# Turning the next chunk's embeddings at the end of the old chunk's last tile, at all three chunk borders of a DLRM interaction kernel

## What is computed

```python
e = stack([tbl_f[ids[:, f]] for f in range(39)], axis=1)          # x0: (512, 39, 16)
for W in (W0, W1):                                                # (1, 39*Hk, 128)
    Wr = W.reshape(39, Hk, 128)                                   # Hk = 39, then 128
    xk = einsum('bid,bjd,ijh->bhd', x0, xk, Wr)
    outs.append(xk)
z = sum(concatenate(outs, axis=1), axis=-1)                       # (512, 256)
h = relu([z, dense_ctx] @ W_top1 + b_top1)                        # 272 -> 512
h = relu(h @ W_top2 + b_top2)                                     # 512 -> 256
y = h @ W_top3                                                    # 256 -> 1
```

## Time and profile before

| | before |
|---|---|
| median of 3 runs | 365.79 us (365.4 to 366.7) |
| profiled execution, time | 365.56 us |
| profiled execution, span of the trace | 363.8 us |
| PE busy | 229.9 us (63%), 1673 matmuls |
| DVE busy | 164.8 us (45%) |
| ACT busy | 158.9 us (44%) |
| POOL busy (gathers) | 98.0 us (27%) |

### The profile page before, as it was taken

The page is one execution under the profiler, slowest core; times in us unless marked ns, Lnnn a source line. Parts: engine busy times, 40 slices in busy tenths (PEclk is TensorE's granted clock), DMA queues, the critical chain, the costliest instruction groups (busy, mean ns, idle before and its releaser), DMA issues.

```text
span 363.8 us, 4707 instructions
## 1 busy us (share of the span) xinstructions
PE 229.9 (63%) x1673; PEld 176.2 (48%) x1673; DVE 164.8 (45%) x333; ACT 158.9 (44%) x307; POOL 98.0 (27%) x107
## 2 busy tenths in 40 slices
PE   5311100010001001889998999989999999999997
PEld 4200000000000000746765887667688877788896
DVE  4440000000000100589897867979784867745411
ACT  4600000000000300488887757986856877666411
POOL 5777777777777730000000000000000000000000
PEclk9655555555555555699999999999999999999999
DMA  6800100000000000019100000000000000000000
GB/s 175 253 14 6 10 6 6 7 7 6 6 7 6 6 5 0 0 31 304 46 21 2 1 2 1 2 0 3 1 2 2 0 3 0 3 0 2 0 2 0
DMA packets 7834, 8.61 MB, mean 24 GB/s; under 512 B 2759, under 2 KB 5420, under 8 KB 7812
## 3 DMA queue, kind: packets, MB, share of 16 engines
q1 hardware_dynamic: 4516, 7.48, 7.2%
q0 software_dynamic: 3296, 0.85, 2.5%
HBM read 8.32 MB, written 0.00 MB: 23 GB/s over the span
## 4 chain that ended last, share of the span: by engine, by line
PE 48%; issue 35%; DVE 7%; ACT 7%; another core or an unknown queue 2%; DMA 1%; ACTq 0%; DVEq 0%
PE turn_bank L542 10%; PE g_bank L512 5%; PE pair_bank L455 5%; PE x_bank L479 5%; PE x_bank L482 4%; PE x_bank L481 4%; DVE onehot L791 3%; ACT prod_hi L1027 2%; DVE prod_lo L864 2%; PE x_bank L522 2%; PE turn_bank L580 2%; PE g_bank L706 2%; PE turn_bank L553 1%; ACT prod L1022 1%
## 5 line engine op out<-in xcount | busy, mean ns | idle before, releaser
L430 POOL DMA_INDIRECT emb<-tbl,ids_sb x103 | 97.8, 950 | 33.5 <-issue 31.1
L1022 ACT ACTIVATE prod<-pair_bank 128x512 f32<-128x512 f32 (+1 forms) x112 | 66.2, 600 | 43.0 <-PE pair_bank L455 38.7
L864 DVE TENSOR_TENSOR prod_lo<-prod,prod_hi 128x512 fp32r<-128x512 f32 x96 | 65.1, 686 | 2.6
L479 PE MATMUL x_bank<-prod_hi,pair_w_hi 128*128 128x512 f32 (+1 forms) x112 | 63.4, 566 | 2.0 <-DVE prod_lo L864 1.9
L1142 ACT ACTIVATE looked<-pair_bank 128x192 f32<-128x192 f32 x2 | 0.6, 328 | 104.4 <-remote 104.4
L808 DVE COPY_PREDICATED looked<-odd,pair_bank 128x192 f32<-128x192 int32 x2 | 0.6, 370 | 97.6 <-issue 97.6
L455 PE MATMUL pair_bank<-x,sel 117*128 117x512 bf16 (+1 forms) x112 | 42.8, 384 | 0.9 <-ACT x L1004 0.7
L542 PE MATMUL turn_bank<-g_sb,w_sb 128*128 128x128 f32 x312 | 42.3, 279 | 0.0
L542 PEld LDWEIGHTS turn_bank<-g_sb,w_sb 128*128 128x128 f32 x312 | 39.4, 192 | 3.0 <-issue 1.2
L1027 ACT ACTIVATE prod_hi<-prod 128x512 fp32r<-128x512 f32 x64 | 40.0, 625 | 0.1
L482 PE MATMUL x_bank<-prod_hi,pair_w_lo 128*128 128x512 f32 x96 | 38.1, 397 | 0.0
(11 more groups left out here) (143 smaller groups left out, 315.2 us busy)
## 6 DMA issues: line engine op xcount, KB each, us to landing
emb<-tbl,ids_sb POOLq DMA_INDIRECT x103
tab<-small SPq DMA_DIRECT2D x2, 560.0 KB
wt<-w_top SPq DMA_DIRECT2D x2, 512.0 KB, 4.4
tab<-small SPq DMA_DIRECT2D x1, 504.0 KB
wa<-pair_w_a SPq DMA_DIRECT2D x1, 448.0 KB
wb<-pair_w_b SPq DMA_DIRECT2D x1, 448.0 KB
wtd<-w_dense SPq DMA_DIRECT2D x1, 256.0 KB
dense_sb<-dense_t SPq DMA_DIRECT2D x1, 256.0 KB
```

Of the source, the lines that this page charges most:

```text
L430: pool.indirect_dma_start(out=emb[:, at:at + D], out_offset=None, in_=tables[f], in_offset=bass.IndirectOffsetOnAxis(ap=ids_sb[:, c * M + ...
L479: mm = pe.matmul(x1_banks[k % 2][:, :], pair_w_hi[p, t, :], hi(n), start=(t == 0), stop=(t == FULL))
L864: dve.tensor_tensor(lo(n), prod[rows, n % RING, :], prod_hi[rows, n % RING2, :], ALU.subtract).then_inc(lo_done, 1)
L1022: act.activation(prod[0:ROWS[t], n % RING, :], pair_bank[n % 2][0:ROWS[t], :], ACT.Square).then_inc(sq_done, 1)
```

## The change

`SEAMS`, `ended` and `seam` are gone, so that all borders are crossed alike. `SPLIT_AT` gets a row for each chunk that is prepared: for each of the two pieces the tile of the last block at which its first half and its second half are issued. For chunk 1 the large piece stays at tiles 4 and 5 and the small one goes to tile 6; for chunks 2 and 3 the large piece is issued at tiles 0 and 1 and the small one at tiles 3 and 4. The turn moves from the new chunk's first tile to the old chunk's last, behind that tile's select and one `layer1`. So it stands ahead of `layer1` of the old chunk's last four tiles; before, two of these stood ahead of it at borders 2 and 3, and all four at border 1. The copies of the turned x move along with it. At border 1 layer 2 of chunk 0 moves from the seam and the first two blocks of chunk 1 to its blocks 2 and 3.

```diff
-SEAMS = (1,)
-SPLIT_AT = (4, 6)
+SPLIT_AT = ((), ((4, 5), (6, 6)), ((0, 1), (3, 4)), ((0, 1), (3, 4)))
...
-            def seam(c):
-
-
-                n, k = c * NB * NT, c * NB
-                for m in range(n - LAG1, n):
-                    layer1(m)
-                    if m % NT in G_AT:
-                        contract_d(k - 2, G_AT.index(m % NT))
-                turn_x1(k - 1)
-                contract_d(k - 1, 0)
-                turn(c, 0)
...
                 late = 1 <= c < NCH and j == 0
                 if late and t == 0:
                     layer1(m)
                     layer1(m + 1)
-                    pe.wait_ge(x1_done, n // NT - 1)
-                    turn(c, 0)
-                    pe.wait_ge(xblk_done, n // NT)
-                    turn(c, 1)
-                    pe.wait_ge(sq_done, n - 1)
-                    turn(c, 2)
-                    layer1(m + 2)
                 if n < TILES:
                     select_pair(n)
                 if m >= 0 and (not late or t >= LAG1):
                     layer1(m)
-                if late and t == 1:
-                    layer1(m + 2)
+                if late and t in (1, 2):
+                    layer1(m + 1)
+                if c + 1 < NCH and j == NB - 1 and t == NT - 1:
+                    pe.wait_ge(x1_done, n // NT)
+                    turn(c + 1, 0)
+                    pe.wait_ge(xblk_done, n // NT + 1)
+                    turn(c + 1, 1)
+                    pe.wait_ge(sq_done, n)
+                    turn(c + 1, 2)
...
-                if c in SEAMS and 13 + 3 * (NT * j + t - LAG1) < M:
-                    layer2(c - 1, 13 + 3 * (NT * j + t - LAG1), min(16 + 3 * (NT * j + t - LAG1), M))
-                if j == 2 and c >= 1 and c not in SEAMS:
+                if j == 2 and c >= 1:
                     layer2(c - 1, 3 * t, 3 * t + 3)
...
(DVE)
-                for p in range(len(SPLIT_AT) - 1):
-                    if splits and t == SPLIT_AT[p]:
+                if splits and t == NT - 1:
+                    take_lo(n - 1)
+                for p in range(len(CUTS) - 1):
+                    if splits and t == SPLIT_AT[c + 1][p][0]:
                         split_rest(c + 1, CUTS[p], CUTS[p + 1])
-                    if splits and t == SPLIT_AT[p] + 1:
+                    if splits and t == SPLIT_AT[c + 1][p][1]:
                         split_lo(c + 1, CUTS[p], CUTS[p + 1])
                 if splits and t == NT - 1:
-
-                    take_lo(n - 1)
...
+                    keep_turned(c + 1)
...
(ACT)
-                    split_first(c + 1, *CUTS[-2:])
-                    split_second(c + 1, *CUTS[-2:])
-                    if c + 1 in SEAMS:
-                        keep_g(k, 0)
-                    else:
-                        round_hi(n)
+                    round_hi(n)
+                    keep_turned(c + 1)
```

More of the change, by code:

```diff
@@ L209, in build_tower @@
         h1_sum = sem("h1_sum")
-        gathered = [[sem(f"gathered{c}_{p}") for p in range(len(SPLIT_AT) if c else 1)] for c in range(NCH)]
+        gathered = [[sem(f"gathered{c}_{p}") for p in range(len(CUTS) - 1 if c else 1)] for c in range(NCH)]
         split_first_done = sem("split_first_done")
@@ L644, in step @@
                     layer1(m)
-                if late and t == 1:
-                    layer1(m + 2)
+                if late and t in (1, 2):
[7 more added lines that the diff above has]
+                    turn(c + 1, 2)
                 if t == 0 and n < TILES:
                     turn_x(n // NT)
-                if u == 0 and k >= 1 and not ended(k - 1):
+                if u == 0 and k >= 1:
                     turn_x1(k - 1)
-                if u in G_AT and k >= 1 and not ended(k - 1):
+                if u in G_AT and k >= 1:
                     contract_d(k - 1, G_AT.index(u))
@@ L919, in step @@
                     spread_x(k)
-                if t == 1 and k >= 2 and not ended(k - 1) and not ended(k - 2):
+                if t == 1 and k >= 2:
                     keep_g(k - 2, 0)
@@ L923, in step @@
                     relu1(c - 2)
-                if t == 4 and k >= 2 and not ended(k - 1) and not ended(k - 2):
+                if t == 4 and k >= 2:
                     keep_g(k - 2, 1)
@@ L1089, in step @@
                 tile(n)
-                if t == 3 and k >= 1 and not ended(k - 1):
+                if t == 3 and k >= 1:
                     keep_x1h(k - 1)
-                if t == 1 and k >= 2 and not ended(k - 1) and not ended(k - 2):
+                if t == 1 and k >= 2:
                     keep_g(k - 2, 0)
-                if t == 4 and k >= 2 and not ended(k - 1) and not ended(k - 2):
+                if t == 4 and k >= 2:
                     keep_g(k - 2, 1)
-                if t == 5 and k >= 1 and not ended(k - 1):
+                if t == 5 and k >= 1:
                     keep_x1(k - 1)
```

32 lines of the change are left out of this document (2 added, 30 removed).

## The result

The changed kernel takes **367.63 us** (median of 5 runs, 367.22 to 367.95), the kernel before 365.79 us. The ratio is 1.004, with a 95% interval of 1.0025 to 1.0054: slower by 1.8 us. The profiled execution took 367.22 us with a span of 365.4 us. In two of the measurements further down one run lay hundreds of us above the others (one of six of after_again, one of twelve of fill12), and in one of the kernel before at 381 us; such runs are left out.

The account below looks back on a forecast made before the run. The prediction took PE (TensorE) to set the pace inside the chunks. Terms of -1.9, -0.6, +2.1, +0.3, +0.3 and a last 0.2 summed to +0.4, forecasting 366.2 us, with a range of 364.9 to 368.3.

Parts of the forecast that it names:

- a clock under 1.00 behind the hole: Sign in the trace after, at border 1: TensorE's clock below full level there would prove the forecast wrong on its sum.
- the clock's rival: At border 1 PE's standing lets the clock fall; four us at half speed lose 2.0, giving 368.2 us; chance 0.2.
- the sum: All gains and losses at the borders and in chunk 1's blocks together: +0.4 us, giving 366.2 us.
- Borders 2 and 3: Early splits and the moved turn remove PE's whole loss at these borders: -1.9 us and -0.6 us.
- The hole: At border 1, PE stands 3.9 us ahead of the turn, waiting for the last split.
- Border 1 in all: Loss at border 1 of 4.7 us in place of 2.6, from the standing, refill and a small gap: +2.1 us.
- The refill term: Behind the turn at border 1, without layer 2 as cover, PE loses 0.7 us to late work (bounds 0 and 1.2).
- Chunk 1's blocks: Blocks 0 and 1 without layer 2 lose 0.3 us; blocks 2 and 3 with it lose 0.3 us.
- The last 0.2: An allowance of 0.2 us for splits that a tile somewhere waits for.
- The other signs: Wait 3.5 to 4.2 us; tile 35's select near 205.8, tile 55's 2.5 to 3 later; borders 2 and 3 3.2 to 3.4.
- Only the hole costs: Rival: ACT and DVE get ahead during border 1's standing, so refill and chunk 1's blocks lose nothing: 364.6 us; chance 0.12.
- The early splits don't help: Rival: borders 2 and 3 don't gain their 2.5 us, as selects or layer 1 still wait: 368.7 us; chance 0.08.

Follow-up runs that it names:

- after_again: The changed kernel unaltered, measured again beside other kernels on one chip: 368.31 us, ratio 1.0064 to the kernel before.
- fill12: The changed kernel with 12 extra matmuls, whose result nobody reads, ahead of the turn at border 1: 366.40 us, ratio 1.0015 to the kernel before.
- fill16: The changed kernel with 16 extra 512-column matmuls, whose result nobody reads, ahead of the turn at border 1: 366.10 us, ratio 1.0009 to the kernel before.
- order1: The changed kernel with layer 1 of tiles 24 and 25 ahead of the turn at border 1 and tile 26's directly behind it: 365.88 us.
- fill8: The changed kernel with 8 extra matmuls, whose result nobody reads, directly behind layer 1 of tile 23: median 367.97 us, ratio 1.0053 to the kernel before.
- split5: The changed kernel with chunk 1's small split at tile 5 instead of 6: 234.93 us against 234.31 for the kernel before (shorter start-up), ratio 1.0011.
- late_splits: The changed kernel with the splits of chunks 2 and 3 at tiles 4, 5 and 6: 240.67 us against 234.31 for the kernel before (shorter start-up).
- seam_kept: The kernel before with the new splits and turn at borders 2 and 3 only, border 1 keeping the old seam: 365.04 us, ratio 0.9981.
- seam_cover: seam_kept with 26 layer 2 matmuls moved from chunk 1's blocks 0 and 1 to its block 3: ratio 0.9936 to the kernel before; repeated, 364.41 us.

## Why the prediction was right, and where it was not

The measured 367.63 lies in the range, but it is near the time of a rival (368.2), not the forecast's 366.2. The prediction named one sign that came true against it: a clock under 1.00 behind the hole. That the range holds the result is owed to its upper end, which was drawn just past the clock's rival, and is no merit of the sum. Point by point:

- **The sum holds.** fill16, in which the clock stays full, is the forecast's case. Its chunks' part is 172.86 - 172.41 = 0.45 us longer than before, where I summed +0.4; the medians say +0.3 (fill16) and +0.5 (fill12).
- **Borders 2 and 3**, forecast -1.9 and -0.6. The layer 1 that moved behind the second select has to be counted in: tiles 55 to 56 gain 2.57 and 83 to 84 1.24, and 56 to 83 and the three tiles behind 84 give back 0.71 each. Net -1.9 and -0.5.
- **The hole**, forecast 3.9: 3.69 as the profile has it, 195.24 less the 191.16 + 0.23 at which the last matmul was over is 3.85.
- **Border 1 in all**, forecast +2.1. Tiles 27 to 35 take 7.18 + 7.99 = 15.17 with the clock full; the two contractions (1.50) and 22 matmuls of layer 2 (4.91) that went to later blocks make it 21.6, against 19.31 before: +2.3. The refill term was about right in size, and order1 confirms its cause, ACT's queue.
- **Chunk 1's blocks**, forecast +0.3 and +0.3: 34.52 less the moved 6.41 is 28.1, against 27.56: +0.55.
- **The last 0.2**, for splits that a tile would wait for, was not there: PE is busy 11.50 of 11.50 us in chunk 1's last block.
- **The other signs.** The hole, the 3.26 us at borders 2 and 3 and the last block of chunk 1 came as forecast. The select of tile 35 stands at 207.08 for the 205.8 forecast, and that of tile 55 is 4.0 us later than before, not 2.5 to 3: the clock again, since in fill16 the first comes 15.17 us after the select of tile 27 (15.1 by the forecast) and the way from tile 27 to 55 is 2.8 us longer than before.
- **The step that failed is the chance of the clock's fall.** The rival's mechanism, place and sign were right: it fell in every run. I gave it 0.2 because the hole was "about equal, not greater" than the one of the start-up. That read one observed fall as if it were a bound. The dense part of the trace of before had no hole over 1 us from which to tell better. By fill8 and split5, holes of 1.95 and 2.4 us already let the clock fall in a part of the executions; at 3.7 us it fell in all ten, so a chance of 0.2 was far too low.
- **The rival's price**, 2.0, was somewhat too high for this trace: 174.29 - 172.86 = 1.43. I priced half of 4.0 us of dense work; here the clock was low from 195.0 to 198.4, and the first 0.2 us of it lay in the hole. Other traces gave 1.5 (after_again) and 2.4 (late_splits).

On this the Trainium skill, page "TensorE: Matmul & The Clock Gate", section "HAM oscillation — how this bites in real kernels", was the better guide than my weighing: it tells of a kernel in which waits of some 3 to 5 us between groups of matmuls make the next group start throttled. The runs here agree for the 3.7 us hole, save that in after_again the fall came 0.9 us into the next group. That the clock also fell in most runs with a hole of 1.95 us goes beyond what the section tells.

The other two rivals fell. "Only the hole costs" needed the refill and the blocks to lose nothing, and they lost what was worked out. "The early splits don't help" is wrong for this kernel, since late_splits is 4.6 us slower; but seam_kept shows the cover that it hangs on, which the prediction had named.

What stays open: why one execution with a given hole has the fall and the next not, and what sets its place and length. Three traces with a hole of 3.7 us have it 3.6 us after the last matmul (the changed kernel), 2.3 us after it (late_splits) and 0.9 us after the hole's end (after_again), and a low clock for 3.4, 6.8 and 3.4 us. No run here tells why.

## What to carry to other kernels

Before moving a step up on the engine that sets the pace, look up when its last input is ready, and leave in front of it the work that doesn't need it: two groups of layer 1 matmuls ahead of the turn, and one behind, were worth some 1.8 us here (367.63 to 365.88), most of it the clock. By the runs here, a wait of about 2 us and more on TensorE in a dense stretch should be priced twice, once for the standing and once for the clock (1.4 to 2.4 us in the three traces with a fall). Work spread early on other engines was free here only as long as the pace-setting engine had filler beside it; move the two together, as seam_cover does.

## What the runs showed of the hardware

TensorE's clock fell to 1.2 GHz at a standing of 3.7 us in all ten runs of the changed kernel (two traces, the rest by their times), at about 2.4 us in six of ten by their times, at 1.95 us in eight of eleven by their times, and at 1.1 us in none that can be told from its time. In the one trace of late_splits two holes of about 1.65 us left it full. The fall came inside the hole or up to 0.9 us behind it, the clock stayed low for 3.4 us or, once, 6.8 us, and that cost 1.4, 1.5 and 2.4 us. Filling the hole with matmuls that nobody needs gave some 1.5 us back, though they do nothing for the result.
